# Last stage of a two-layer attention and FFN kernel: the rounded running maxima are loaded into row 0 of the mask's operand, and one product per half gives mask and log decay

## The reference, cut to what matters

```
lf      = concat(0, cumsum(log_sigmoid(f_pre)))
log_d   = lf[t+1] - lf[s+1] + i_pre[s]           # -inf where s > t
m       = max over s of log_d
d_mat   = exp(log_d - m)
scores  = q @ k.T / sqrt(32)
s_mat   = scores * d_mat
denom   = max(|sum_s s_mat|, exp(-m)) + 5e-5
h       = (s_mat @ v) / denom
h       = h * rsqrt(mean(h*h) + 1e-6) * gain      # per head
```

## Time and profile before

| | us |
|---|---|
| median of 3 runs | 419.32 |
| the three runs | 419.77, 414.97, 419.32 |
| span of the profiled execution, first to last instruction | 414.9 |
| PE busy in the span | 335.8 (81%) |
| DVE busy | 305.9 (74%) |
| ACT busy | 263.8 (64%) |
| POOL busy | 183.8 (44%) |

### The profile page before, as it was taken

The page is one execution under the profiler, slowest core; times in us unless marked ns, Lnnn a source line. Parts: engine busy times, 40 slices in busy tenths (PEclk is TensorE's granted clock), DMA queues, the critical chain, the costliest instruction groups (busy, mean ns, idle before and its releaser), DMA issues.

```text
span 414.9 us, 9157 instructions
## 1 busy us (share of the span) xinstructions
PE 335.8 (81%) x3093; PEld 236.8 (57%) x3093; DVE 305.9 (74%) x1025; ACT 263.8 (64%) x567; POOL 183.8 (44%) x207
## 2 busy tenths in 40 slices
PE   2999589998999999823678787779488999999864
PEld 2777467776776777502345555446265666666421
DVE  2798735777889988676997999985436777787751
ACT  1565335466445455735788898886668888888520
POOL 2114300212212465139997899982005555445520
PEclk9999989999999999955979999999889999999986
DMA  7499999979653640000000000000001222222000
GB/s 251 122 283 303 299 217 214 257 136 266 128 105 88 130 42 2 1 0 0 2 1 2 0 2 2 2 0 2 0 14 28 38 53 53 46 46 39 28 25 25
DMA packets 43869, 33.68 MB, mean 81 GB/s; under 512 B 19888, under 2 KB 39728, under 8 KB 43696
## 3 DMA queue, kind: packets, MB, share of 16 engines
q1 hardware_dynamic: 43824, 33.11, 32.7%
HBM read 24.71 MB, written 8.39 MB: 80 GB/s over the span
## 4 chain that ended last, share of the span: by engine, by line
PE 55%; DVE 18%; issue 13%; ACT 7%; POOL 4%; DMA 2%; SPq 1%; DVEq 0%; POOLq 0%; ACTq 0%
PE PS L1461 5%; PE PS L1238 5%; PE PS L1227 4%; DVE sm L741 4%; PE PS L1296 4%; PE PS L1451 4%; PE PS L1218 4%; PE PS L1217 4%; PE PS L1157 4%; PE PS L1257 3%; PE PS L1446 3%; PE PS L1424 3%; ACT pT L991 2%; DVE sm L713 2%; PE PS L1414 2%
## 5 line engine op out<-in xcount | busy, mean ns | idle before, releaser
L991 ACT ACTIVATE pT<-PS 128x512 f32<-128x512 f32 x64 | 36.6, 596 | 50.8 <-PE PS L1218 50.5
L606 DVE TENSOR_REDUCE negm<-PS 128x4 bf16<-128x512 f32 x64 | 42.3, 683 | 15.6 <-PE PS L1227 15.5
L435 POOL TENSOR_TENSOR sm<-sm,mhalf 128x1 f32<-128x1 f32 x16 | 11.3, 708 | 83.8 <-DVE sm L638 83.8
L451 POOL TENSOR_TENSOR kst<-kst,rows 128x1024 f32<-128x1024 f32 x16 | 37.6, 2351 | 8.1 <-ACT kst L1059 8.0
L1103 ACT ACTIVATE lnT<-PS,Atok 128x128 f32<-128x128 f32 x128 | 36.4, 368 | 3.7 <-DVE lnb L849 2.0
L1336 PE MATMUL PS<-identf,w2f 128*128 128x128 f32 x128 | 19.2, 297 | 20.6 <-ACT w2f L1048 20.6
L1218 PE MATMUL PS<-identb,negm 128*128 128x128 bf16 x256 | 35.6, 222 | 0.0
L465 POOL TENSOR_TENSOR kst<-kst,rows 128x1024 f32<-128x1024 f32 x14 | 33.1, 2363 | 0.0
L1238 PE MATMUL PS<-pT,vx 128*32 128x128 f32 x512 | 27.3, 287 | 5.0 <-ACT pT L991 5.0
L1336 PEld LDWEIGHTS PS<-identf,w2f 128*128 128x128 f32 x128 | 15.2, 151 | 24.9 <-ACT w2f L1048 19.6
L1461 PE MATMUL PS<-wd,xT 128*128 128x392 f32 x64 | 27.0, 548 | 1.8 <-DVE rest L885 1.8
(11 more groups left out here) (220 smaller groups left out, 977.7 us busy)
## 6 DMA issues: line engine op xcount, KB each, us to landing
scr_q<-qpart SPq DMA_DIRECT2D x8, 384.0 KB, 3.9
scr_k<-kpart SPq DMA_DIRECT2D x8, 384.0 KB, 4.7
X<-in_x SPq DMA_DIRECT2D x8, 256.0 KB, 4.5
CTXT<-in_ctxT SPq DMA_DIRECT2D x8, 256.0 KB, 4.7
vx<-in_ctx SPq DMA_DIRECT2D x16, 128.0 KB, 3.0
out<-rest SPq DMA_DIRECT2D x16, 128.0 KB, 1.7
rows<-in_rows SPq DMA_DIRECT2D x1, 1544.0 KB, 8.9
qst<-scr_q SPq DMA_DIRECT2D x8, 192.0 KB, 4.4
```

The lines of the kernel that those rows point to most:

```text
L451: gp.tensor_tensor(n2[q.slot], n2[q.slot], ln2g, ALU.mult).then_inc(b_g2, 1)
L606: v.tensor_reduce(negm[f.slot % 2][:, 4 * hg:4 * hg + 4], PS[:, 2 + hg % 2, :].rearrange("p (h k) -> p h k", h=4), AX_X, ALU.max, negate=T ...
L991: s.activation(pT[:, hg, :], PS[:, hg % 2, :], ACT.Exp, scale=float(DH0) ** -0.5).then_inc(a_e, 1)
```

## The change

- DVE rounds -M once to bf16, into `Mb`. What the rounding lost is `resg` = -M - Mb. The two further parts, `sel`, `rowsel`, `place`, `MPARTS` and their two evictions are gone.
- `masks` [128, 32, 128] holds 32 copies of the mask: a head of one of four batches each. In the mask, row 0 is zero. SP loads 8 rows of `Mb` (one batch, 256 bytes a row) into row 0, partition 0, of the eight copies of slot b % 4. The first four batches are one transfer of 32 rows, issued when `Mb` is ready; from batch 4 on there is one transfer per batch, issued two turns ahead.
- `onerow` is the identity with a row 0 of ones. One product `onerow` x `masks` (512 columns) gives mask and -M together: `log_d` is one matmul and not five.
- The exponent used is a(s) + Mb(t), which is off by resg(t) for all s. Numerator and sum have the same factor exp(-resg), so `EM` is formed with Mb and 5e-5 is multiplied by `EF` = exp(-resg). For that PE transposes `Mb` and `resg` in place of `MT`, ACT makes `EF` with one exponential, and DVE's L912 becomes a `scalar_tensor_tensor`.
- SP issues the contexts of batches 0 and 1 before it waits for `Mb`.
- POOL writes `onerow` and `masks` in place of `sel` and `rowsel`: a cast of 128 elements a partition, two small memsets, the mask, and one copy that spreads the mask over the 31 other places (3968 elements a partition).

```diff
-        sel = sb("sel", [128, PARTS, NB, 4, H1], BF16)
-        rowsel = sb("rowsel", [128, 4 * H1], BF16)
+        masks = sb("masks", [128, 4 * H1, 128], BF16)
+        onerow = sb("onerow", [128, 128], BF16)
@@ SP
+            def load_maxima(b):
+                done(sp, c_arg, Turn(b, 0, 0), -3, 2)
+                sp.dma_start(masks[0:1, b % 4 * H1:(b % 4 + 1) * H1, :],
+                             Mb[b * H1:(b + 1) * H1, :]).then_inc(m_ld[b % 4], 16)
             def turn_cd(n, _a, _b, _c, _e, d):
-                if n:
+                if n and n.b >= 2:
                     load_c(n)
+                    if n.b + 2 < NB:
+                        load_maxima(n.b + 2)
                 if d:
                     store_out(d)
+            for b in range(2):
+                load_c(Turn(b, b, 0))
+            sp.wait_ge(g_m, 1)
+            sp.dma_start(masks[0:1, :, :], Mb[0:4 * H1, :]).then_inc(m_first, 16)
@@ POOL
+            step(gp.tensor_copy(onerow[:], identf[:]))
+            step(gp.memset(onerow[0:1, :], 1.0))
+            step(gp.memset(masks[:, 0, :], 0.0))
+            step(gp.affine_select(out=masks[:, 0, :], in_=masks[:, 0, :], ...
-            step(gp.memset(sel[:], 0.0))
-            for k in range(PARTS):
-                step(gp.tensor_copy(sel[:, k, :, k, :], identf[:]...
-            step(gp.memset(rowsel[:], 0.0))
-            for k in range(4): ... affine_select ...
+            step(gp.tensor_copy(masks[:, 1:, :], masks[:, 0:1, :].to_broadcast([128, 4 * H1 - 1, 128])))
@@ DVE
-            v.tensor_scalar(part[:, 0, :], MT[:], -1.0, None, ALU.mult).then_inc(g_m, 1)
+            v.tensor_scalar(Mb[:], MT[:], -1.0, None, ALU.mult).then_inc(g_m, 1)
             ... resg as before, from Mb ...
-            v.tensor_copy(part[:, 1, :], resg[:]).then_inc(g_m, 1)
-            v.tensor_tensor(part[:, 2, :], resg[:], part[:, 1, :], ALU.subtract).then_inc(g_m, 1)
-                    if a.b == 0:
-                        dve.wait_ge(g_sel, 2)
-                        v.tensor_copy(MPARTS[:, 1:4, :], PS[:, 7, 0:3 * S]...).then_inc(g_MR, 1)
-                    b_den = cc.mark(v.tensor_scalar(den[:, :, 2], den[:, :, 1], 5e-5, None, ALU.add))
+                    b_den = cc.mark(v.scalar_tensor_tensor(out=den[:, :, 2], in0=EF[:, b.b, :], scalar=5e-5,
+                                                           in1=den[:, :, 1], op0=ALU.mult, op1=ALU.add))
@@ ACT
-            act.wait_ge(g_sel, 1)
-            s.activation(MPARTS[:, 0, :], PS[:, 5, 0:S], ACT.Copy).then_inc(g_MP, 1)
+            act.wait_ge(g_tp, 3)
+            s.activation(EF[:]..., PS[:, 6, 0:128], ACT.Exp, scale=-1.0).then_inc(g_act, 1)
@@ PE
-            t.transpose(PS[:, 3, 0:128], MT[:], identf[:]).then_inc(g_tp, 1)
-            pe.wait_ge(g_m, 4)
-            place(0, 5, 0).then_inc(g_sel, 1)
+            pe.wait_ge(g_m, 1)
+            t.matmul(PS[:, 3, 0:128], Mb[:], identb[:], start=True, stop=True).then_inc(g_tp, 1)
+            pe.wait_ge(g_m, 2)
+            t.transpose(PS[:, 6, 0:128], resg[:], identf[:]).then_inc(g_tp, 1)
 def log_d(half):
+                    if half == 0 and n.used:
+                        pe.wait_ge(m_ld[n.slot], 16 * n.used)
+                    elif half == 0:
+                        pe.wait_ge(m_first, 16)
                     ...
-                    t.matmul(bank, identb[:], maskb[:].unsqueeze(1).to_broadcast([128, 4, 128]), start=True, stop=False)
-                    for j in range(4):
-                        last = t.matmul(bank[:, j * 128:(j + 1) * 128], rowsel[:, hs + j:hs + j + 1].to_broadcast([128, 128]),
-                                        MPARTS[:, n.used, :], start=False, stop=(j == 3))
+                    last = t.matmul(PS[:, half, :], onerow[:], masks[:, hs:hs + 4, :], start=True, stop=True)
@@ PE, after the scores of batch 0
-                        for q in range(1, 4):
-                            last = place(q, 7, (q - 1) * S)
```

More of the change, by code:

```diff
@@ L125, in build @@
         identf = sb("identf", [128, 128]); identb = sb("identb", [128, 128], BF16)
-        upper = sb("upper", [128, 128]); maskb = sb("maskb", [128, 128], BF16)
+        upper = sb("upper", [128, 128]); masks = sb("masks", [128, 4 * H1, 128], BF16)
         onesf = sb("onesf", [128, 128]); mhalf = sb("mhalf", [128, H1])
-        sel = sb("sel", [128, PARTS, NB, 4, H1], BF16)
-        rowsel = sb("rowsel", [128, 4 * H1], BF16)
+        onerow = sb("onerow", [128, 128], BF16)
         wabs = sb("wabs", [128, 2]); wmean = sb("wmean", [128, 2])
@@ L229, in build @@
         resg = sb("resg", [128, S])
-        part = sb("gpart", [128, PARTS, S], BF16)
-        Atok = sb("Atok", [128, NB, H1]); MPARTS = sb("MPARTS", [128, 4, S], BF16)
+        Mb = sb("Mb", [128, S], BF16)
+        Atok = sb("Atok", [128, NB, H1]); EF = sb("EF", [128, NB, H1])
         gcol = sb("gcol", [2 * H1, 1]); warm = sb("warm", [128, 1])
@@ L235, in build @@
         g_th = sem("g_tanh_ready"); g_act = sem("g_scalar_steps"); g_pe = sem("g_sums_ready")
-        g_e = sem("g_u_less_one_ready"); g_sel = sem("g_parts_placed"); g_A = sem("g_log_inputs_ready")
-        g_I = sem("g_input_gates_ready"); g_MP = sem("g_max_parts_ready"); g_MR = sem("g_max_rest_ready")
-        g_m = sem("g_max_parts_chain")
+        g_e = sem("g_u_less_one_ready"); g_A = sem("g_log_inputs_ready")
+        g_I = sem("g_input_gates_ready"); g_m = sem("g_max_rounded")
+        m_first = sem("m_first_rows_loaded"); m_ld = [sem(f"m_rows_loaded{i}") for i in range(4)]
         vx2 = [sb(f"vx2{i}", [128, H1, 64]) for i in range(2)]
@@ L404, in _ @@
                                   pattern=[[1, 128]], channel_multiplier=-1))
-            step(gp.memset(maskb[:], 0.0))
-            step(gp.affine_select(out=maskb[:], in_=maskb[:], compare_op=ALU.is_ge, fill=-30000.0, base=0,
+            step(gp.tensor_copy(onerow[:], identf[:]))
+            step(gp.memset(onerow[0:1, :], 1.0))
+            step(gp.memset(masks[:, 0, :], 0.0))
+            step(gp.affine_select(out=masks[:, 0, :], in_=masks[:, 0, :], compare_op=ALU.is_ge, fill=-30000.0, base=0,
                                   pattern=[[1, 128]], channel_multiplier=-1))
-            step(gp.memset(sel[:], 0.0))
-            for k in range(PARTS):
-                step(gp.tensor_copy(sel[:, k, :, k, :], identf[:].rearrange("p (b h) -> p b h", b=NB)))
-            step(gp.memset(rowsel[:], 0.0))
[L414 to L417, removed]
+            step(gp.tensor_copy(masks[:, 1:, :], masks[:, 0:1, :].to_broadcast([128, 4 * H1 - 1, 128])))
             for i in range(2):
@@ L820, in _ @@
             link(v.tensor_tensor_scan(MT[:], aT[:], aT[:], -3.0e38, ALU.max, ALU.max))
-            v.tensor_scalar(part[:, 0, :], MT[:], -1.0, None, ALU.mult).then_inc(g_m, 1)
+            v.tensor_scalar(Mb[:], MT[:], -1.0, None, ALU.mult).then_inc(g_m, 1)
             dve.wait_ge(g_m, 1)
-            v.scalar_tensor_tensor(out=resg[:], in0=MT[:], scalar=-1.0, in1=part[:, 0, :],
+            v.scalar_tensor_tensor(out=resg[:], in0=MT[:], scalar=-1.0, in1=Mb[:],
                                    op0=ALU.mult, op1=ALU.subtract).then_inc(g_m, 1)
-            dve.wait_ge(g_m, 2)
-            v.tensor_copy(part[:, 1, :], resg[:]).then_inc(g_m, 1)
-            dve.wait_ge(g_m, 3)
-            v.tensor_tensor(part[:, 2, :], resg[:], part[:, 1, :], ALU.subtract).then_inc(g_m, 1)
             dve.wait_ge(g_pe, 2)
@@ L834, in _ @@
             link(v.tensor_copy(Mt[:], PS[:, 3, 0:128]))
-            v.tensor_tensor(Mt[:], PS[:, 2, 0:128], Mt[:], ALU.subtract).then_inc(g_pre, 1)
+            v.tensor_tensor(Mt[:], PS[:, 2, 0:128], Mt[:], ALU.add).then_inc(g_pre, 1)
             SC1 = float(DH1) ** -0.5
@@ L870, in turn_cd @@
                     weights(1)
-                    if a.b == 0:
-                        dve.wait_ge(g_sel, 2)
-                        v.tensor_copy(MPARTS[:, 1:4, :], PS[:, 7, 0:3 * S].rearrange("p (g s) -> p g s", g=3)).then_inc(g_MR, 1)
                 if c:
@@ L911, in turn_cd @@
                     dve.wait_ge(c_ch, b_abs)
-                    b_den = cc.mark(v.tensor_scalar(den[:, :, 2], den[:, :, 1], 5e-5, None, ALU.add))
+                    b_den = cc.mark(v.scalar_tensor_tensor(out=den[:, :, 2], in0=EF[:, b.b, :], scalar=5e-5, in1=den[:, :, 1],
+                                                           op0=ALU.mult, op1=ALU.add))
                 if c:
@@ L1086, in _ @@
             s.activation(warm[:], th[:, 0, 0:1], ACT.Exp)
-            act.wait_ge(g_sel, 1)
-            s.activation(MPARTS[:, 0, :], PS[:, 5, 0:S], ACT.Copy).then_inc(g_MP, 1)
+            act.wait_ge(g_tp, 3)
+            s.activation(EF[:].rearrange("p b h -> p (b h)"), PS[:, 6, 0:128], ACT.Exp, scale=-1.0).then_inc(g_act, 1)
             act.wait_ge(g_pre, 2)
@@ L1426, in turn_cd @@
                     last.then_inc(c_s, 1)
-                    if a.b == 0:
-                        for q in range(1, 4):
```

(4 more changed lines are left out.)

11 lines of the change are left out of this document (removed).

## The result

The changed kernel takes 420.3 us in the median of 12 runs (418.81 to 422.78); the kernel before takes 417.55 in the median of 12 (414.97 to 419.77; the 419.32 ahead of the prediction was the median of three of them). The ratio is 1.009, 95% interval 1.0065 to 1.0116. Timed once more in a later comparison it was 1.006 (1.0021 to 1.0098). By the mark of 2% this is no change; by the interval it is slower. I had forecast a gain of 1.8 us. The ratios of this document leave out executions more than 1.5% above the fastest of their kernel; that takes out four of the ten of experiment e1, so that its ratio looks better than its median.

The account below looks back on a forecast made before the run. PE was taken to bound the full turns, with a loop without log_d just behind at 5.62 us. Full turns (-1.25) and stage start (-0.56) summed to -1.8 us, so 419.3 became 417.5 us, range 412.0 to 420.5.

Parts of the forecast that it names:

- Bound of the full turns: Last stage, eleven full turns: each falls from 5.74 us to a floor of 5.62 set by a loop without log_d.
- PE's 99% share: Full turns before the change: PE's busy share, cited as the argument for PE being the bound.
- L912's 17 ns: Full turns: the new scalar_tensor_tensor on DVE costs 17 ns more a turn, 0.2 us lost over eleven.
- Start up to the first weights: Start of the last stage, rounding to end of first weights: 0.56 us gained.
- L: Start of the last stage: time of the first row transfer from SBUF to SBUF, taken as 2.0 us.
- the two wake-ups: Start of the last stage: SP and PE waking around the first transfer, 0.11 us in all.
- POOL's constants ... Nothing, with 13 us of cover: Early POOL setup, from near 41.5 us: the mask copy, at most 16.9 us, hides in idle time and costs nothing.
- The nine placed products ... off the chain: nothing: Second turn of the last stage: removing these products and a DVE eviction, beside and after the weights, changes nothing.
- The clock stays low longer: Rival, first turns of the last stage: one at 1.2 GHz costs 1.8 us, two 3.7; 419.3 or 421.2; chance 0.15.
- PE is the bound: Rival, full turns: all 0.44 us a turn is gained, 4.8 us in eleven; 413.7 us; chance 0.10.
- the row transfer is slow: Rival, start of the last stage: a transfer above 3.8 us makes the kernel slower; 419.5 at 4.0; chance 0.13.
- The level: Whole kernel: the gain of 1.8 us taken unchanged from the median 419.3 us, giving 417.5.

Follow-up runs that it names:

- e1: Changed kernel with POOL's mask copy held back until DVE has written the last q and k parts; 418.03 us, ratio 0.9992.
- e5: Changed kernel with the product of the first half of log_d issued twice; one run, 417.86 us.
- e10: Changed kernel with two instead of four exponentials in the second half of each turn; one run, 419.05 us.
- e13: e1 once more, the changed kernel with POOL's copy held back; 418.5 us, ratio 1.0034 to the kernel before.
- e15: e13 plus two unread 512-column products behind the scores of the first batch; 415.35 us, ratio 0.9976.
- e14: e13 plus three unread 512-column products during the first transfer; 417.47 us, ratio 1.0009.
- e7: e6 plus unread products before PE's waits in the turns without scores at the end; 411.48 us, ratio 0.9862.
- e2: Kernel before with an added, unused POOL copy of the mask to 32 places; 418.3 us, ratio 1.0037.
- e3: Changed kernel with POOL's one long mask copy split into 31 copies of 128 elements; one run, 419.61 us.
- e12: The changed kernel itself timed again, beside the kernel before; 419.07 us, ratio 1.006.
- e4: Changed kernel, POOL's copy held back, with five unread products: three during the first transfer, two behind the first scores; 414.68 us, ratio 0.9953.
- e6: Changed kernel, POOL's copy held back, with unread products in every PE gap of the gate stage and behind the first scores; one run, 412.87 us.
- e9: Changed kernel with POOL's power for the row block of c made a multiplication; one run, 419.67 us.
- e11: Changed kernel with both the cuts of e9 and e10; one run, 411.19 us.

## Why the prediction was wrong, step by step

- **Bound of the full turns: right.** Forecast 5.62 us, measured 5.61, and e5 and e10 show that it is not PE's and that POOL's loop has that length; the read-off from the turns without log_d was the right one, and PE's 99% share was not. The eleven turns gained 1.54 us for 1.3 less 0.2. L912's 17 ns were not paid: 148 ns before, 0.15 us after.
- **Start up to the first weights: right.** L was 1.84 us for 2.0, the two wake-ups 0.06 for 0.11, and the weights began 2.27 us behind the first product, as forecast (2.28). The gain was 0.78 us for 0.56.
- **"POOL's constants ... Nothing, with 13 us of cover": the first step that failed.** I asked how long the copy lasts and who waits for its result. The length was safe (3.49 us; the bound was 16.9, and the estimate of 6 beside it was too long as well). I did not ask whom the instruction holds while it runs. The trace before even hinted at it: L878, with both inputs in SBUF, has a median of 0.41 us and takes 0.82 once, at 392.64, while a POOL operation runs from 392.50 to 393.18. One pair of traces has 2.3 us for it, seven against seven 1.4, the timings 0.6 to 1.5. It does not explain the sign alone: with the copy moved (e13) the ratio is still 1.0034.
- **"The nine placed products ... off the chain: nothing": the second step that failed, and the dearer one.** Two unread products in their place (e15 against e13) are worth 3.2 us of medians or 0.6%, with intervals that overlap, and the rise of the clock comes 5.6 us behind the rounding instead of 10.1. The sum had no term for the clock.
- **"The clock stays low longer" (0.15): this rival came true**, in its size too: 0.88 + 0.45 + 0.47 = 1.8 us in the first turn, as worked out for one cold turn. Its cause was named too narrowly: I looked at the wait for the transfer. The rule of the Trainium skill cited in that place ("TensorE: Matmul & The Clock Gate", section "HAM oscillation — how this bites in real kernels") bears on this. The trace agrees in part: the clock was low for longer once a transfer stood in front of the products (10.3 us behind the rounding for 5.5), but filling the wait for the transfer alone did not bring it back (e14, 15.6), and closing a gap that was no wait for a transfer did (e15, 5.6).
- **The end of the kernel was in no term.** It lost 1.8 us to a clock that fell by 397 us instead of 400, in turns that the change does not touch. e7 shows that the low clock costs it. About 0.6 of the 1.8 is the short return of the clock in the one profile of the kernel before; e2, which is that kernel with the copy, has no such return and takes 27.9 us for this stretch. The point at which the clock falls moves between executions (394.3 to 403.2 us in the profiled ones), but it is more regular when counted in products behind gtT. In before and e2 it lies 1.3 and 1.9 us behind the 14th of the 16. In six profiles of the changed kernel in which nothing was added for PE (changed, e1, e3, e12, e13, and e10 with its shorter exponentials) it lies 1.5 to 2.2 us behind the 13th, one turn earlier. In the other profiles in which it falls near here (e4, e5, e6, e9, e11, e14, e15) it lies 0.2 to 1.9 us behind the 14th again. So the earlier fall goes with the change in most executions; why is open.
- **The two rivals "PE is the bound" and "the row transfer is slow"** were excluded by 5.61 and 1.84.
- **The level.** 417.5 came from adding the gain to a median of three runs; the range ended at 420.5, and 420.3 is inside it. That is luck: the upper end stood for a transfer of 5.0 us, or for one cold turn with a transfer of 3.0, and the transfer took 1.84. The sign was wrong.

The sum in the profiles: -1.54 in the turns, -0.78 at the start, +1.57 left over in the first turns, where the clock is, +2.26 ahead of the gate stage, +1.8 at the end, together +3.3 us. The medians differ by 2.75.

## What to carry to other kernels

Cost a moved or merged constant not only by who needs it and when, but by which engine its instruction holds up while it runs; a long POOL copy belongs where DVE reads PSUM, or in pieces. Where several loops stand within a few per cent of each other, look for turns in which the work in question is absent: they give the next bound directly. Work off the chain that keeps TensorE busy had a value of its own here while the clock was about to rise; when such work is taken out, try what unread products in its place bring back.

## What the runs showed of the hardware

- One POOL copy of 3968 bf16 elements a partition took 3.49 us (0.88 ns an element) and held a DVE operation with two SBUF inputs until its end: 3.07 us for 0.70; a copy of 4096 elements took 3.60 and held it for 2.57. Split into pieces of 128 elements it cost DVE nothing, while POOL's 21 first pieces stretched over 9.23 us.
- A transfer from SBUF to SBUF of 32 rows of 256 bytes into one partition took 1.84 us in every profile (1.84 to 1.86).
- Device time was 1.7 to 1.9 us above the span from first to last instruction (1.9 to 3.0 in e7).
- Executions of one kernel with a lower granted clock are mostly longer: in e1's ten runs 412.57 us has 0.943 and 420.83 has 0.915.
- The clock came back at 2.4 GHz 5.4 to 6.4 us behind the rounding in five traces with products beside the first scores, and 8.9 to 15.6 us behind it in nine without.
